# Moving half of a small load from the SyncE queue to the ScalarE queue in a one-core decoder layer

## The reference

```python
x = x + attn(layernorm(x)); x = x + xattn(layernorm(x), ctx); x = x + ffn(layernorm(x))
# attn, per head, over the tokens:
M = M * exp(g_t)
M = M + k_t (v_t - k_t M)^T b_t
o_t = q_t M
```

## Time and profile before

| what | value |
|---|---|
| median of three runs | 2053.12 us |
| profiled execution | 2074.74 us |
| its span, first to last instruction | 2072.9 us |
| y16 of head 0 to y16 of head 15 | 1444.4 us |
| PE busy | 1967.5 us, 95% of the span |
| DVE, ACT, POOL busy | 56%, 44%, 36% of the span |
| mean granted TensorE clock | 0.942 of full speed |

### The profile page before, as it was taken

The page is one execution under the profiler, slowest core; times in us unless marked ns, Lnnn a source line. Parts: engine busy times, 40 slices in busy tenths (PEclk is TensorE's granted clock), DMA queues, the critical chain, the costliest instruction groups (busy, mean ns, idle before and its releaser), DMA issues.

```text
span 2072.9 us, 41974 instructions
## 1 busy us (share of the span) xinstructions
PE 1967.5 (95%) x14914; PEld 1599.8 (77%) x14914; DVE 1164.2 (56%) x2080; ACT 915.3 (44%) x2923; POOL 737.6 (36%) x1151
## 2 busy tenths in 40 slices
PE   5899999999999999999999999999998799999999
PEld 3688888888888888888888888888887575657574
DVE  6657565565757475656566565757473443434433
ACT  2555463636555454636463635545453321312121
POOL 1345362525445353626362535445353100000000
PEclk8999999989999799979999989999797899999999
DMA  3011120201011110101110101011013512112110
GB/s 99 21 32 39 25 46 15 40 20 35 20 35 32 24 42 18 38 17 40 25 40 20 35 20 35 25 30 43 13 34 136 142 41 82 51 60 72 42 39 20
DMA packets 220094, 85.43 MB, mean 41 GB/s; under 512 B 138320, under 2 KB 204240, under 8 KB 219280
## 3 DMA queue, kind: packets, MB, share of 16 engines
q1 hardware_dynamic: 220048, 84.83, 16.2%
HBM read 57.28 MB, written 27.53 MB: 41 GB/s over the span
## 4 chain that ended last, share of the span: by engine, by line
PE 70%; issue 18%; DVE 4%; POOL 4%; ACT 3%; DMA 1%; POOLq 0%; DVEq 0%; ACTq 0%; SPq 0%
PE bank L566 30%; PE bank L893 4%; PE bank L699 3%; PE bank L841 2%; PE bank L735 2%; PE bank L835 2%; PE bank L850 2%; PE bank L771 2%; PE bank L857 2%; PE bank L724 2%; PE bank L956 1%; PE bank L974 1%; PE bank L675 1%; PE bank L856 1%; PE bank L648 1%
## 5 line engine op out<-in xcount | busy, mean ns | idle before, releaser
L566 PE MATMUL bank<-x_hi,w_hi 128*128 128x512 f32 x1024 | 425.4, 415 | 8.2 <-DVE kT L1430 6.1
L566 PE MATMUL bank<-x_lo,w_hi 128*128 128x512 f32 x1024 | 412.2, 403 | 0.0
L566 PE MATMUL bank<-x_hi,w_lo 128*128 128x512 f32 x1024 | 411.9, 402 | 0.0
L566 PEld LDWEIGHTS bank<-x_hi,w_hi 128*128 128x128 f32 x1024 | 197.4, 193 | 48.7 <-DVE kT L1430 6.5
L566 PEld LDWEIGHTS bank<-x_hi,w_lo 128*128 128x128 f32 x1024 | 194.5, 190 | 39.0
L566 PEld LDWEIGHTS bank<-x_lo,w_hi 128*128 128x128 f32 x1024 | 196.7, 192 | 35.2
L1430 DVE SCALAR_TENSOR_TENSOR qT<-bank,cw,qT 128x511 f32<-128x511 f32 (+2 forms) x192 | 141.9, 746 | 51.1 <-ACT qT L1076 46.6
L1813 POOL TENSOR_TENSOR qT<-qT,gam 128x512 f32<-128x512 f32 x48 | 59.9, 1276 | 290.4 <-PE bank L699 290.4
L1856 POOL TENSOR_TENSOR rstd<-ve,mhalf 128x1 f32<-128x1 f32 x32 | 17.4, 543 | 387.0 <-DVE ve L1611 387.0
L1230 ACT ACTIVATE o_tmp<-bank 128x128 f32<-128x128 f32 x256 | 67.2, 277 | 198.6 <-PE bank L857 198.6
L1430 DVE SCALAR_TENSOR_TENSOR kT<-bank,cw,kT 128x511 f32<-128x511 f32 (+2 forms) x192 | 143.2, 746 | 9.0 <-ACT kT L1076 4.0
(11 more groups left out here) (222 smaller groups left out, 4533.6 us busy)
## 6 DMA issues: line engine op xcount, KB each, us to landing
w_raw<-in_w_heads SPq DMA_DIRECT2D x64, 256.0 KB, 2.8
o_d<-og SPq DMA_DIRECT2D x64, 256.0 KB, 2.6
o_raw<-o_d SPq DMA_DIRECT2D x16, 1024.0 KB, 6.1
x_in<-in_x SPq DMA_DIRECT2D x16, 256.0 KB, 3.3
blkN_d<-nT SPq DMA_DIRECT2D x64, 64.0 KB, 2.0
t<-blkT_d SPq DMA_DIRECT2D x64, 64.0 KB, 2.3
wo_raw<-in_w_out SPq DMA_DIRECT2D x4, 1024.0 KB, 8.9
x_res<-in_x SPq DMA_DIRECT2D x16, 256.0 KB, 2.8
```

Source lines behind the costliest of these rows:

```text
L566: last = mm(bank[bk][:, :], w[:, kind % 2, d, :], xx[:, d, b * S:(b + 1) * S], start=(n == 0), stop=(n == 3 * ND - 1))
```

## The change

SP loads only the first two of the four tiles (`k` = 0, 1). ACT loads the other two (`k` = 2, 3): it waits for `blkT_out` and issues the two DMAs, between its `q_squares(3)` and `keep16_y`. All four still add to `t32_in`, and those who wait for `t32_in` still wait for 64 a head.

```diff
@@ sync, head
                 sp.wait_ge(blkT_out, 32 * h + 32)
-                for k in range(NPAIR):
+                for k in range(NPAIR // 2):
                     sl = slice(k * PAIR, (k + 1) * PAIR)
                     sp.dma_start(t32[sl, :, :, sl].rearrange("t b c s -> t (b c) s"),
                                  blkT_d[k].rearrange("u t s -> t u s")).then_inc(t32_in, 16)
@@ scalar, head
+                act.wait_ge(blkT_out, 32 * h + 32)
+                for k in range(NPAIR // 2, NPAIR):
+                    sl = slice(k * PAIR, (k + 1) * PAIR)
+                    act.dma_start(t32[sl, :, :, sl].rearrange("t b c s -> t (b c) s"),
+                                  blkT_d[k].rearrange("u t s -> t u s")).then_inc(t32_in, 16)
                 keep16_y()
```

## The result

| | before | after |
|---|---|---|
| median of the runs timed side by side (19 each) | 2061.29 us | 2075.37 us |
| lowest and highest | 2043.26 to 2083.82 us | 2065.71 to 2083.29 us |
| ratio after / before | | 1.008, interval 1.005 to 1.010 |
| profiled execution, its span | 2074.74, 2072.9 us | 2072.41, 2070.7 us |
| mean granted clock of the profiled execution | 0.942 | 0.950 |

The change makes no difference of 2%. The forecast was 2150 us, 75 us too much, and the range (2098 to 2190) missed.

The account below looks back on a forecast made before the run. The prediction took PE, busy 95% of the span, to bound the kernel. It summed 2074.7 + 45 (later y16) + 37 (clock) = 2157 us, took off a third of 21.6 and forecast 2150 us, range 2098 to 2190.

Parts of the forecast that it names:

- The step that failed: ACT's two loads in head 4: issued only after the last squares end, at 510.14 and 510.63 us.
- the low bound: Shift of y16: at least 1.9 us a head, with issue 0.4 us earlier and the minimum landing of 2.0 us.
- The whole shift: PE's start of y16 moves later by 2.8 us a head, 45 us over sixteen heads.
- the 3 us below which the prediction called itself wrong: Sign at PE's wait before y16: a gap staying under 3 us refutes the prediction, which expected about 4.4.
- The second step: Granted clock over the heads: the wider gap before y16 costs 2.5 us a head more, 37 us in all.
- the fourth: Rival at ACT's loads: issued before the squares are through, or landing in under 0.3 us; 2053 to 2075 us, chance 0.02.
- The third rival: Clock at y16: the gap absorbs the fall, clock returns before the joins, gaining up to 73 us; 2047 us, chance 0.10.
- the 73 us of the clock: Windows from y16 to y16 before the change: lowered clock costs 73 us over the heads, 4.9 a head.

Follow-up runs that it names:

- the kernel with the early loads: The kernel after, with ACT's two loads and the wait for blkT_out moved ahead of rhs0(3); 2063.85 us, ratio 1.0055.
- The kernel without a gap: The kernel before, with PE's last q transposes before v's, ACT's last squares ahead of rhs0(3) and z silu, nv_done wait moved to z16; 1981.55 us, ratio 0.966.
- the squares first: The kernel before with its last q transposes and squares moved earlier, plus two loads on ACT right behind q_squares(3); 2059.4 us, ratio 1.001.

## Why the prediction was wrong

What held. The load was not on the path before; SP gained nothing; the wait for `blkT_out` and the two issues cost ACT nothing, as the kernel with the early loads shows; the landing took 2.3 us from the second issue by the median of the heads, as taken; DVE's transposes stayed hidden; and PE's wait at y16 passed from the squares to the load.

**The step that failed** is "The two DMAs then go out at 510.14 and 510.63", and with it the low bound, by which the sequencer could be 0.4 us ahead of the arithmetic. I had read the end of ACT's arithmetic as the time at which its stream gets to the next item. The sequencer was 2.2 us ahead. What the squares wait for could be seen in the trace of before, in head 4:

```profile
507.29 0.60 PE L665 MATMUL bank<-ident,qT 128*128 128x128 f32 x4
```

These last transposes of q end at 507.89. With 0.06 us for the step and 0.34 between the issues, both from the trace of after, 2.3 for the landing and 0.14 until PE starts, y16 comes at 510.7 instead of 510.44: 0.3 us, where 0.4 was measured. The whole shift was 7.7 us at equal clock and not 45. The kernel whose loads do wait for the squares is the counterproof, with 41. PE's gap of 2.0 us is also under the 3 us below which the prediction called itself wrong.

The Trainium skill (Advanced Engine Details and Errata, Engine Queue Depths) gives ScalarE a queue of 8 on this chip. When the load of head 4 went out at 505.90, the second activation of `rhs0` was under way and two more, the z silu and four squares had yet to start, eight activations in all. That alone would fit into the 8. But the trace lists behind each square a read of the accumulator as an instruction of its own, which makes twelve and is more than the 8 if the reads take a place; whether they do, and whether a longer row of work would hold the load back, no run here shows.

**The second step** is "I take half of the way from the mean of today to the worst kind, 2.5 us a head, 37 us". The mean clock didn't fall at all (0.9476, 0.9494). In part this hangs on the first step, since the gap it priced was 4.4 us and the real one is 2.0; at 4.2 us the clock did cost 35 us. The sentence ahead of it, that "a longer idle time makes the fall more certain and puts it earlier", is borne out as far as it goes: 13 of the 15 windows have a low stretch at 1.6 us, 14 at 2.0 and all at 2.55 and 4.2, and at 4.2 the clock falls before y16 begins (in head 4 it is 0.74 from 545 to 546 us, and y16 starts at 546.23). What doesn't follow from it is more time at the low clock. The windows with the longest stretch, 24 us, are five at 1.6 us, two at 2.0, none at 2.55 and six at 4.2, in one execution of each.

**The rival that came nearest** is the fourth, "the change doesn't bite: ACT issues its two loads before the squares are through", at 2053 to 2075 us. It has the time (2075.37) and the cause right, but it held that PE's wait would then not change, and the load is issued before the squares are through and still comes last. I gave it 0.02 and held it nearly excluded by the order of the stream and by the landing time. The order tells in which sequence the items are handed out and not how far handing out runs ahead of finishing, and no row of before has a DMA on ACT's queue in a head. A price without a row asks for wide bounds, and mine went only from 1.9 to 3.1 us. The third rival had the clock come back behind a longer gap; in these runs it is a shorter one, of 1.15 us or less, that brings it back.

The prediction also took the 73 us of the clock as given, and left open whether the gap or the small tiles of y16 bring it. The kernel without a gap runs the same tiles and loses nothing in its windows. The 1.6 us of idleness ahead of them were what cost, 26 us by themselves and 62 through the clock.

## What to carry to other kernels

A DMA that stood behind arithmetic in ACT's stream was issued, in every kernel here, when the last semaphore wait ahead of it was met; put such a DMA in time by that wait, and if it has to follow the arithmetic, it needs a semaphore that the arithmetic raises. Before you judge a load that moves, write down all that the waiting engine waits for at that point and by how much each comes ahead: at equal clock the same edit cost 7.7 us here and 24 us, 78 with the clock, where the other awaited thing was early. Where executions of one kernel spread with the granted clock, compare at equal clock first, and then look for a short gap on PE that returns in every pass, since closing it may give more than its length.

## What the runs showed of the hardware that was not expected

- ACT's queue issued its DMA 0.06 to 0.07 us after the last wait ahead of it was met, 2.2 us before the activations ahead of it had ended, in all 16 heads of the kernel after; the step is the same with one load, with three, with the loads early and with the squares first. An issue took it 0.31 to 0.51 us, as on SP.
- A gap of 1.1 us before the small tiles left the mean clock at 0.978, one of 1.6 us brought it to 0.95, and 2.55 us (0.955) no lower. With 0.1 us no window of a head lost any clock. The low stretch is PE at 1.2 GHz, and its length varies between heads with the same work: it is short in the windows of 0.98 and long in those of 0.88. What picks the length is open; identical heads in identical kernels differ in it, and so do two executions of one kernel.
- The Trainium skill (TensorE: Matmul & The Clock Gate, HAM oscillation) tells of a loop that waits for a transfer on each pass and runs each pass throttled. The kernel whose loads wait for the squares agrees in part: with 4.2 us of idleness in each pass all its windows are below full clock, most of them at 0.96 or 0.87 in turn, so no pass is free of it, yet none is throttled throughout.
- Nearly all of the spread between executions of the kernel before (2040 to 2085 us) is the clock: carried to equal clock its runs scatter by 1.9 us (standard deviation), so that the mean of 45 has an error of 0.3, and the kernel whose heads don't lose the clock repeats within 5 us.
